# A fused adapter-attention and expert-layer kernel: unit 0's bias by a matmul, a fourth x buffer, residuals in halves, another order around the convolution, the last pair in three column parts

## The reference, cut to what matters

```python
def reference(x, cond, fside, ...):
    # 1: a weight matrix and a bias per batch, mixed by a small softmaxed MLP of cond
    att = softmax(mlp(cond))                                    # 32 x 8
    z = einsum('boi,bih->boh', einsum('bk,koi->boi', att, W), x) + (att @ bias_k)[:, :, None]
    # 2: causal attention over 64 tokens, 32 heads of 32, plus 10 adapter tokens
    q, k, v = split(z @ w_attn.T); q, k = rope(q), rope(k)
    y = softmax(mask(q @ k.T / sqrt(32))) @ v + gate * softmax(q @ ak.T / 32) @ av
    x = x + y @ w_proj.T
    # 3: grouped convolution over channels (9 taps, 4 groups) with a bias per batch
    c = conv1d(x, conv_w, groups=4) + (cond @ c_weight.T)[:, :, None] + fside
    # 4: base layer plus the best two of eight low-rank experts
    w = top2_softmax(c @ W_router.T)
    return x + c @ W_base.T + b_base + 2 * sum_e w_e * (c @ A_e.T) @ B_e.T
```

## Time and profile before

| | us |
|---|---|
| median of three runs | 1213.07 |
| the three runs | 1211.04, 1213.07, 1213.1 |
| the profiled execution, its device time | 1210.89 |
| its span, first to last instruction | 1209.1 |
| device time outside the span | 1.8 |

### The profile page before, as it was taken

One profiled execution on the slowest core, in us unless ns is written; L12 is line 12 of the kernel. 1 busy time (PEld: TensorE's weight loads), 2 busy tenths in 40 slices (PEclk: granted clock), 3 DMA queues, 4 the chain that ended last, 5 costly groups with the idle time before them and its releaser, 6 DMA issues.

```text
span 1209.1 us, 19478 instructions
## 1 busy us (share of the span) xinstructions
PE 1188.6 (98%) x7934; PEld 1035.2 (86%) x7934; DVE 735.1 (61%) x1480; ACT 384.4 (32%) x701; POOL 53.9 (4%) x25
## 2 busy tenths in 40 slices
PE   6999999999999999999999999999999999999997
PEld 5978888888888888888888887899999999999997
DVE  4977857777777777768668598533333333333332
ACT  3534443544535445344444465210001111100000
POOL 1000000000000000000000000100111000000001
PEclk9999999999999999999999999999999999999999
DMA  7412001001001002001020425322222222222221
GB/s 229 158 36 70 10 18 62 10 19 61 19 10 62 19 9 71 10 15 66 9 70 10 156 90 193 118 89 89 90 102 96 91 90 89 90 100 97 94 78 42
DMA packets 58533, 85.81 MB, mean 71 GB/s; under 512 B 5946, under 2 KB 44366, under 8 KB 57550
## 3 DMA queue, kind: packets, MB, share of 16 engines
q1 hardware_dynamic: 58446, 84.58, 20.8%
HBM read 59.38 MB, written 25.18 MB: 70 GB/s over the span
## 4 chain that ended last, share of the span: by engine, by line
PE 95%; DVE 2%; SPq 1%; issue 1%; DMA 1%; ACT 0%; DVEq 0%; ACTq 0%
PE psum L787 43%; PE psum L871 17%; PE psum L844 14%; PE psum L856 4%; PE psum L739 3%; PE psum L770 3%; PE psum L755 2%; PE psum L246 2%; PE psum L891 2%; PE psum L799 2%; PE psum L808 1%; PE psum L748 1%; PE psum L764 1%; SPq L583 0%; DMA m_x<-in_x 0%
## 5 line engine op out<-in xcount | busy, mean ns | idle before, releaser
L787 PE MATMUL psum<-z,w_hi 128*128 128x512 f32 x1536 | 481.6, 395 | 0.0
L787 PEld LDWEIGHTS psum<-z,w_hi 128*128 128x128 f32 x1536 | 282.5, 188 | 55.5
L787 PE MATMUL psum<-z,w_lo 128*128 128x512 f32 x768 | 300.1, 391 | 0.0
L787 PEld LDWEIGHTS psum<-z,w_lo 128*128 128x128 f32 x768 | 144.1, 188 | 31.5
L1047 ACT ACTIVATE a_kbd<-a_kr 32x512 f32<-32x512 f32 x128 | 80.6, 630 | 225.5 <-DVE a_kr L1160 224.4
L710 POOL TENSOR_TENSOR f_x1b<-f_x,_bbase 128x1024 f32<-128x1024 f32 x16 | 49.2, 3077 | 1105.0 <-DVE a_aprob L1210 717.7
L1174 DVE TENSOR_TENSOR a_prob<-psum,a_mask 128x512 f32<-128x512 f32 x64 | 43.9, 685 | 87.6 <-PE psum L739 87.6
L871 PE MATMUL psum<-f_wfhi,f_chi 128*128 128x388 f32 (+1 forms) x384 | 94.0, 339 | 1.9 <-DVE f_osb L1299 1.5
L871 PE MATMUL psum<-f_wflo,f_chi 128*128 128x388 f32 (+1 forms) x384 | 93.6, 338 | 0.0
L871 PE MATMUL psum<-f_wfhi,f_clo 128*128 128x388 f32 (+1 forms) x384 | 93.5, 338 | 0.0
L1267 DVE COPY f_lg<-psum 128x8 f32<-128x8 f32 x16 | 2.7, 167 | 131.4 <-PE psum L871 131.4
(11 more groups left out here) (153 smaller groups left out, 1641.7 us busy)
## 6 DMA issues: line engine op xcount, KB each, us to landing
w_st<-in_wqkvT SPq DMA_DIRECT2D x7, 1536.0 KB, 6.8
m_x<-in_x SPq DMA_DIRECT2D x16, 512.0 KB, 3.5
y_scratch<-a_ysb SPq DMA_DIRECT2D x32, 256.0 KB, 2.5
f_yst<-y_scratch SPq DMA_DIRECT2D x16, 512.0 KB, 4.5
f_xt<-in_x SPq DMA_DIRECT2D x16, 512.0 KB, 3.7
x_scratch<-f_x SPq DMA_DIRECT2D x16, 512.0 KB, 2.6
_x<-x_scratch SPq DMA_DIRECT2D x128, 64.0 KB, 2.6
out<-f_osb SPq DMA_DIRECT2D x16, 512.0 KB, 2.7
```

Source lines behind the costliest of these rows:

```text
L787: mm = pe.matmul(dst, w[:, c, x, :], zs, start=(c == 0 and i == 0), stop=(c == KC - 1 and i == 2))
```

## The change

- **Start.** `aggb_diag` (DVE) spreads the bias rows of unit 0's 8 batches over a block diagonal of 8 x 512. One matmul of `ones` (8 x 128) with it, behind the L234 matmuls on PE, gives unit 0's bias on all partitions in bank 3, and ACT copies it to `aggb[0]` between its two halves of `aggT` copies. ACT's copy of the bias rows now waits for `aggb_diag`. SP no longer loads `aggb[0]`. There is a fourth x buffer, in the place of `vbd`; `vbd` is cleared later on POOL. SP loads pairs 2 and 3 right behind the store of the bias rows, pair 4 ahead of the ten constants (L583), and then the V weights and pairs 5 and on.
- **Unit 0 to 1.** `high` and `low` of the last pair move: on ACT behind the adapter's key copies (`akbd`), on DVE into unit 1.
- **Passage.** Residuals of pairs 0 and 1 are added in two halves; pair 1 is projected into banks 7 and 5 and starts when the first half of pair 0's residual is done. Its projection is no longer split around the last unit's transposes. `convolve(0)` goes ahead of the last `attend_values`, which now writes bank 6, and PE then waits for the copy of that result (`y_copied`) before it goes on to pair 2's projection. DVE makes the fourth `wflo` ahead of `convolved(0)`.
- **Pair loop.** PE: `turn_hidden`, `convolve(p+1)`, `low_rank`, then all the rest of the projection. DVE: `convolved(p+1)` ahead of `finish(p)`.
- **Last two pairs.** `convolve(15)` goes into the middle of pair 14's last column part. The convolution's parts of pair 15 go into `yhi` and `ylo`, so they wait for the last projection instead of for pair 14's last layer. Pair 15 is finished and stored in three column parts, each when its `low_rank` part is done.

```diff
@@ mixing, Sync.begin @@
-            Sync.load_x(sp, 2)
+            for i in range(2, NX):
+                Sync.load_x(sp, i)
             sp.wait_ge(aggb_out, 16)
-            for u in range(NU):
+            for u in range(1, NU):
                 sp.dma_start(aggb[u][:], ...)
-                if u == 0:
-                    Sync.load_w(sp, Q_)
-            Sync.load_w(sp, V_)
+            Sync.load_w(sp, Q_)
@@ mixing, Tensor.begin, behind the L234 matmuls @@
+            pe.wait_ge(aggb_spread, 1)
+            pe.wait_ge(ctx_set, 1)
+            pe.matmul(turned_bank[:], ones[:], aggb_diag[:].rearrange("p b o -> p (b o)"), start=True, stop=True
+                      ).then_inc(aggb_wide, 1)
@@ mixing, Scalar.begin @@
             act.wait_ge(aggb_mm, 1)
+            act.wait_ge(aggb_spread, 1)
             act.activation(aggb_rows[:], small_bank[0:NB, 256:256 + NC], ACT.Copy).then_inc(aggb_copied, 1)
...
+                if i0 == 0:
+                    act.wait_ge(aggb_wide, 1)
+                    act.activation(aggb[0][:], turned_bank[:], ACT.Copy).then_inc(aggb_in[0], 16)
@@ mixing, Vector.begin, behind att_sel @@
+            dve.wait_ge(aggb_mm, 1)
+            dve.tensor_tensor(aggb_diag[:], ..., ALU.mult).then_inc(aggb_spread, 1)
@@ program @@
-            ... [place(t) for t in (x8, prob[0], pT[0])],
+            ... [place(t) for t in (x8, prob[0], pT[0], vbd)],
 def y_bank(m):
-            return bY if m < NG * NU - 1 else bV
+            return bY if m < NG * NU - 1 else bK
+        def proj_banks(p):
+            return (bV, bQ) if p == 1 else (bQ, bK)
@@ sync @@
             mix_sync.begin(sp)
+            mix_sync.load_x(sp, 4)
             for dst, src in (... ten constants ...):
                 sp.dma_start(dst[:], d[src]).then_inc(consts, 16)
-            for i in range(3, NP):
+            mix_sync.load_w(sp, V_)
+            for i in range(5, NP):
                 mix_sync.load_x(sp, i)
...
+            def store_last():
+                for i, k in enumerate((2, 0, 1)):
+                    n0, n1 = cuts[k][1], min(cuts[k][2], L)
+                    sp.wait_ge(part_set, i + 1)
+                    sp.dma_start(out[NB - 2:NB].rearrange("b c l -> (b c) l")[:, n0:n1], osb[:, n0:n1]).then_inc(stored, 16)
@@ tensor @@
 def project_out(p, c0, c1):
-                    wait(pe, x1_set, p)
+                    if p == 1:
+                        pe.wait_ge(x1_half, 1)
+                    else:
+                        wait(pe, x1_set, p)
...
             project_out(0, 0, KC)
             attend_scores(m, NG)
-            project_out(1, 0, 6)
+            pe.wait_ge(vbd_set, NG * NU)
+            project_out(1, 0, KC)
             attend_transposes(m)
-            project_out(1, 6, KC)
-            attend_values(m, NG)
+            pe.wait_ge(ashifted, NG * NU)
+            pe.wait_ge(y_copied, NG * NU - 1)
             pe.wait_ge(fconsts, 16 * NFCONST)
             pe.wait_ge(edges, 2)
             convolve(0)
+            pe.wait_ge(x1_set, 1)
+            attend_values(m, NG)
+            pe.wait_ge(y_copied, NG * NU)
             project_out(2, 0, 2)
 def pair_step(p, ahead):
-                    c0, c1, c2 = (2, 5, 6) if p == 0 else (0, 3, 5)
+                    c0, c1 = (2, 5) if p == 0 else (0, 3)
                     project_out(p + 2, c0, c1)
-                    if p == 0:
-                        pe.wait_ge(y_copied, NG * NU)
                     turn_hidden(p)
-                    project_out(p + 2, c1, c2)
+                    convolve(p + 1)
                     low_rank(p)
-                    convolve(p + 1)
-                    project_out(p + 2, c2, KC)
+                    project_out(p + 2, c1, KC)
                     return
                 for k in (2, 0, 1):
                     if k == 1:
                         turn_hidden(p)
                     for c in range(KC):
                         last_layer(p, (k,), c)
-                if ahead == 1:
-                    convolve(p + 1)
-                low_rank(p)
+                        if ahead == 1 and k == 1 and c == 4:
+                            convolve(p + 1)
+                        if ahead == 0 and k == 1 and c == 3:
+                            low_rank(p, (2, 0))
+                low_rank(p, (1,) if ahead == 0 else (2, 0, 1))
@@ scalar and vector: split_conv, convolved @@
-                wait(dve, ffn_mm, p)
+                if p < NP - 1:
+                    wait(dve, ffn_mm, p)
+                else:
+                    dve.wait_ge(proj_mm, NP)
@@ vector @@
 def residual(p):
+                for n, src in enumerate(proj_banks(p)):        # p < 2; one op as before from p = 2
+                    add = dve.tensor_tensor(x1 half n, src, xt half n, ALU.add)
+                    if p == 0 and n == 0:
+                        add.then_inc(x1_half, 1)
+                add.then_inc(x1_set, 1)
+            def finish_last():
+                for i, k in enumerate((2, 0, 1)):
+                    dve.wait_ge(lora_mm, 2 * (NP - 1) + i + 1)
+                    dve.tensor_tensor(osb[:, n0:n1], bF[:, at:at + n1 - n0], x1b[:, n0:n1], ALU.add).then_inc(part_set, 1)
 def pair_step(p, ahead):
                 router(p)
-                if ahead >= 2:
-                    finish(p)
                 if ahead >= 1:
                     convolved(p + 1)
-                if ahead < 2:
                     finish(p)
+                else:
+                    finish_last()
                 if ahead >= 2:
                     residual(p + 2)
```

More of the change, by code:

```diff
@@ L1059, in unit_step @@
                 if n == 0:
-                    for i in range(NP - 2, NP):
-                        mix_scalar.high(act, i)
+                    mix_scalar.high(act, NP - 2)
                 if att:
```

77 lines of the change are left out of this document (55 added, 22 removed).

## The result

| | before | after |
|---|---|---|
| median of seven runs, us | 1213.07 (1211.04 to 1213.18) | 1203.60 (1201.87 to 1207.16) |
| ratio, with its 95% interval | | 0.9929 (0.9914 to 0.9943) |
| the profiled execution | 1210.89 | 1202.29 |
| its span | 1209.1 | 1200.5 |

The account below looks back on a forecast made before the run. PE bounds the kernel, busy 1188.6 of 1209.1 us. Gains 0.1 + 1.2 + 0.7 + 0.4 + 0 + 1.4 + 0.5 = 4.3 give 1206.6 or 1208.8 by level; forecast the middle, 1207.6, range 1203.3 to 1211.2.

Parts of the forecast that it names:

- the first rival: Start: clock stays up or pair 5 lands early, gain 2.9 instead of 0.1; total 7.1, 1204.8 us; chance 0.15.
- At most 20.5 us can go without taking work from PE: Whole kernel: PE is busy for 1188.6 of 1209.1 us, and the change takes no work from it.
- Start, bias: Start: DRAM trip hidden behind slow `mix(0)`, replacing it worth nothing by itself; filled gap may raise PE's clock sooner.
- Start, x: Start: pair 3's 2.9 wait goes, pair 5 is late next; with the clock charge the start gains 0.1.
- the charge of 1.9 for the clock: Start: a pause of over 3 us since `mix(4)` lowers PE's clock, costing 1.9 (0 to 2.5).
- One wait of about 3 for pair 5: Start: sign that the prediction is right, PE waiting about 3 us for pair 5, ahead of 30.
- Unit 0 to 1: Between units 0 and 1: the last pair's low part leaves PE's 2.3 wait; gain 1.2, at least 0.9.
- Passage: Passage: waits of 0.9 and 1.0 go, 0.7 for ACT's copy and 0.5 for later parts come; net 0.7.
- Step 0 and the loop: Pair loop: step 0's 0.4 wait goes; steps 1 to 13 gain 0, bounds -1 to +1.
- The slower rival: Pair loop: PE's new sequence or POOL's late add costs over 0.35 per step; 1214.9 us; chance 0.04.
- Pair 14: Last two pairs: PE's 1.5 wait behind the low parts; gain 1.4, at least 1.0 if `x8` is late.
- End: End: last add 0.97 becomes 0.55, store 0.2 less, split costs 0.1; gain 0.5, from 0.3 to 1.1.

Follow-up runs that it names:

- bias_dma: Changed kernel with unit 0's bias by way of DRAM again, without the block diagonal and its matmul; 1204.89 us, ratio 0.9940.
- bias_dma_fill: Changed kernel with unit 0's bias by way of DRAM, block diagonal and matmul kept but their result unused; 1205.94 us, ratio 0.9947.
- after_again: The changed kernel unaltered, measured a second time; 1204.50 us, ratio 0.9935.
- values_first: Changed kernel with the last attend_values back ahead of convolve(0) and the fourth wflo behind convolved(0) on DVE; one run, 1203.01 us.
- tail_old: Changed kernel with pair 15 finished as before: low_rank whole, two adds, one store of 512 KB; one run, 1202.89 us.
- start_old: Changed kernel with the old start: bias by way of DRAM, three x buffers, pair 3 behind the ten constants; 1204.87 us, ratio 0.9943.
- consts_pool: Changed kernel with the ten constants issued by POOL instead of SP; 1201.95 us, ratio 0.9916.
- after_fill: Changed kernel with eight idle matmuls of 128 columns in the opening MLP's gaps; 1207.58 us, ratio 0.9956.
- loop_old: Changed kernel with the old pair loop order on PE and DVE for pairs 0 to 13; one run, 1204.17 us.

## Why the prediction was right and where it was off

The direction, the places and most of the sizes were right; the total between the two profiles was twice the forecast. The time, 1203.6, lies at the low edge of the range (1203.3), near the first rival (1204.8), "the start's gain is kept", to which the prediction gave 0.15. 8.6 - 4.3 = 4.3 were missed: start 2.2, steps 1 to 13 1.1, the end 0.7, step 0 0.2, pair 14 0.2, less 0.1 for the passage.

"At most 20.5 us can go without taking work from PE" took PE's busy time for a fixed amount of work. It isn't: 3.7 us of it went, 2.4 of them in the start by a rate that was higher sooner.

**Start, bias.** Right that the trip through DRAM was hidden in the kernel before, and right that it was so behind a slow `mix(0)`: bias_dma, with the load landed 1.4 ahead of the first add, and bias_dma_fill, with the add waiting for the load, show it. `mix(0)` was to end between 16.2 and 18.0; it ended at 16.1, where DVE's first add starts, but at 18.5 in after_again. The sentence that the filled gap may raise the clock sooner is neither borne out nor refuted (see bias_dma_fill).

**Start, x.** Right that pair 3's wait goes and that pair 5 is late next: it was to be issued at 22.5 to 24.3 and was at 21.5, and it landed at 27.03, in the range of 26.9 to 28.7. That it lies in the range is luck: the issue came 1.0 sooner than the range allowed, and the transfer took 5.5 where 4.4 was reckoned. The low part of pair 3 was no bound, as said. The step that failed is the charge of 1.9 for the clock. It was put on a pause "since `mix(4)`, for over 3 us"; but pair 4, issued as soon as `mix(0)` ended, landed only at 22.74, so `mix(4)` ran in the middle of the pause and left 1.75 and 2.10, and behind these the clock stayed. One wait of about 3 for pair 5 was the sign to look for; there were two shorter ones. Without the charge the working gives 31.6 - 29.6 = 2.0, and 2.3 was measured. The charge is real in other executions: bias_dma paid it with mix 5 (3.76 in place of 2.02) and the projections behind it, and values_first paid 1.6 of it with the changed start itself. So the step was wrong in taking it as certain, and the profiled execution that it was held against is among the better ones.

That the moment of the clock isn't the kernel's to set ("TensorE: Matmul & The Clock Gate", section "What's actually happening", in the Trainium skill) was borne out otherwise than it was used: not as a fixed price, but as a spread. Two profiles of one program differ by 2.6 us at the first projection, and over the fourteen profiled executions the matmuls reach the full rate anywhere between about 12 and 20.5 us. The kernel before has the spread too, from 1210.18 to 1213.43 over all comparisons, with a mean clock of 0.999 in its quickest executions, the profiled one among them, and of 0.996 or 0.997 in most others. So its median lies 2.2 above its profiled execution, and the changed kernel's 1.3 (1203.60 against 1202.29): the medians are 9.5 apart, the profiles 8.6.

**Unit 0 to 1.** 1.2 forecast, 1.2 measured: the wait is 2.3 before and 1.07 after, and it is 1.1 in every kernel of this study.

**Passage.** 0.7 forecast, 0.6 measured, with each of its four terms to be seen in PE's waits: 0.9 and 1.0 gone, 0.7 for the copy, 0.6 for the low part (charged 0.5). values_first shows that the last two could have been spared. The prediction held the copy's wait for needed, since bank 6 is used next.

**Step 0 and the loop.** The 0.4 went, and 0.6 was measured: PE's busy time fell by another 0.2, of which one re-entry less explains 0.08. "Nothing that is moved there can gain", said of a stretch in which PE is 100% busy, is the sentence that was wrong. A busy share of 100% says that PE doesn't wait, and not that its sequence has one price. The bound given, -1 to +1 over thirteen steps, missed 1.1 by a little; the value taken, 0, by all of it. It could have been asked of the trace of before: a piece of 18 records takes 4.12 and one of 12 takes 2.77, so 6 records cost 1.35 and a piece has some 0.07 of its own, an estimate; thirteen pieces fewer make 0.9. The changed kernel's one piece of 30 takes 6.82, which is 0.07 + 30 x 0.225. The slower rival, a longer step, fell: POOL's add in step 13 ended at 1163.69 and the residual that needs it came at 1165.04, 1.3 to spare where 0.6 was reckoned.

**Pair 14.** 1.4 forecast, 1.6 measured: 1.5 of wait; PE's busy time is 17.90 against 17.94, although the last layer is now cut once more. `x8` was not late: its last issue ended at 1173.33, and the convolution began at 1176.04 without a wait.

**End.** 0.5 forecast, 1.2 measured, just above the bound of 1.1: the add is 0.4 shorter as said; the store was put at 0.2 less and is 0.8 less between the profiles of before and after, 0.5 to 0.6 against tail_old. The Trainium skill ("DMA: Bandwidth & Descriptors", section "Anatomy of one DMA") gave 0.7 at the very most, an estimate; its fixed cost of about 2.0 is stated there for DMAs that GpSimd issues, and these come from SP. The trace has 2.1 for 194 KB beside 2.8 for 512, a difference of 0.7. The 0.1 for splitting PE's part was 0.04.

## What to carry to other kernels

An engine that is busy for all of a stretch can still be made faster there: look up what the same records cost in one piece and in several before calling it bound. At a start, ask of each early step what it lets the others do; here a matmul brought the bias in time for mixes at full rate, where its load did not, and a load that was moved ahead uncovered the next one in the queue. Where the clock is at stake, don't charge a fixed price: find which transfer lands inside the pause, and give the spread of both outcomes to the range. And take more than one profile of a start before its gain is called shown: five of this one differ by 2.7 us.

## What the runs showed of the hardware

- The rate of the first matmuls isn't in the clock column: in the windows of 15 to 16 us two executions of the same program are both granted 1.00, and one has 12 records, the other 6. Read the records, not the column, at a start.
- PE's pauses of 2.9 to 4.7 us in the start ended in a stretch at 0.50 or were followed by one (before, start_old, bias_dma, bias_dma_fill, consts_pool, after_fill). Shorter ones went both ways: 2.36 (after_again, 31 to 32 us at 0.50) and 2.56 (values_first) were followed by one; 2.78 (bias_dma_fill, the first of its two), 2.54 (loop_old), 2.30 (tail_old) and 2.10 (after) were not.
- The moment at which the first matmuls reach the full rate differs from run to run: about 13 us in after and 20.5 in after_again, which are the same program. It comes with 2.6 us at the first projection.
- Going back to an interrupted matmul sequence cost 0.08 us: 30 records took 6.82 in one piece and 6.90 in two.
- A transfer of 512 KB took 3.7 us from its issue behind the small constants (before), and 6.7 (after) and 8.3 (consts_pool) when loads of bias rows and weights had been issued ahead of it.
- With the last store at 3/8 of 512 KB the end of the span came 0.5 to 0.8 us sooner behind the last add.
